# Token combinations of a first pass moved from one place in every step to two of three steps and into the downs, their low halves from GpSimd to VectorE

## The reference

```
x = x + tanh(g_ffn[0]) * _L0_ffn_ref(_layernorm(x, axis=-1), g_codes, g_absmax, ..., d_lora_b)

DM, DFF, R = (1024, 2752, 16)
w = NF4[codes].reshape(o, i // BLOCK, BLOCK) * absmax[:, :, None]      # Wg, Wu, Wd
y1 = x1 @ Wg + x1 @ g_lora_a @ g_lora_b
y2 = x1 @ Wu + x1 @ u_lora_a @ u_lora_b
x3 = jax.nn.relu(y1) * y2
y3 = x3 @ Wd + x3 @ d_lora_a @ d_lora_b
```

## Time and profile before

| | |
|---|---|
| time, median of 3 runs | 2003.04 us (2002.95 to 2003.74) |
| the profiled execution | 2003.48 us, span 2001.5 us |
| TensorE busy | 1918.8 us, 96% of the span |
| VectorE, ScalarE, GpSimd busy | 65%, 63%, 42% |
| granted TensorE clock, mean | 0.989 |
| HBM traffic | 303 MB, 151 GB/s |

### The profile page before, as it was taken

The page is one execution under the profiler, slowest core; times in us unless marked ns, Lnnn a source line. Parts: engine busy times, 40 slices in busy tenths (PEclk is TensorE's granted clock), DMA queues, the critical chain, the costliest instruction groups (busy, mean ns, idle before and its releaser), DMA issues. The chain is left out here.

```text
span 2001.5 us, 26467 instructions
## 1 busy us (share of the span) xinstructions
PE 1918.8 (96%) x9140; PEld 963.6 (48%) x9140; DVE 1293.8 (65%) x2204; ACT 1254.9 (63%) x1998; POOL 835.4 (42%) x752
## 2 busy tenths in 40 slices
PE   6996888999999999999999999999998899999998
PEld 5774334444444444444444445444444455555554
DVE  5776888364564736555473644636379988888872
ACT  6995668886777677676777776677524343443431
POOL 2443884222223223232232333222268667667742
PEclk9997998999999999999999999999999999999999
DMA  5651545856637375573737556373531110111001
GB/s 201 223 171 55 193 163 195 292 193 215 232 122 265 105 257 190 178 249 127 265 109 252 192 172 227 99 253 117 210 137 59 32 41 29 53 53 38 27 22 42
DMA packets 91989, 303.01 MB, mean 151 GB/s; under 512 B 11984, under 2 KB 16720, under 8 KB 73168
## 3 DMA queue, kind: packets, MB, share of 16 engines
q1 hardware_dynamic: 91856, 301.32, 44.3%
HBM read 274.01 MB, written 27.26 MB: 151 GB/s over the span
## 5 line engine op out<-in xcount | busy, mean ns | idle before, releaser
L1036 ACT ACTIVATE first<-first 128x512 f32<-128x512 int32 x1008 | 625.7, 626 | 27.4 <-DVE wt L1439 1.8
L1265 POOL TENSOR_TENSOR gu<-wt,gu 128x512 f16<-128x512 f32 x86 | 102.3, 1190 | 370.6 <-ACT gu L1055 370.5
L1439 DVE SCALAR_TENSOR_TENSOR wt<-first,w_scale,absm 128x512 f32<-128x512 f32 x132 | 102.6, 777 | 227.4 <-ACT first L1036 226.8
L1785 PE MATMUL a_psQ<-z,gu 128*128 128x512 f16 x936 | 208.5, 379 | 0.0
L2386 PE MATMUL a_psL<-z,l_x 128*128 128x512 f16 x768 | 170.7, 379 | 1.0 <-DVE l_x L2488 0.8
L1785 PE MATMUL a_psC<-z,gu 128*128 128x512 f16 x732 | 167.8, 379 | 0.0
L1785 PE MATMUL a_psC<-z 128*128 128x512 f16 x684 | 156.9, 379 | 0.0
L1785 PEld LDWEIGHTS a_psQ<-z,gu 128*128 128x128 f16 x936 | 91.5, 98 | 110.5
L1277 POOL TENSOR_TENSOR hid_lo<-z,hid_hi 128x512 f16<-128x512 f32 x76 | 90.2, 1201 | 118.7 <-ACT hid_hi L1096 118.6
L1265 POOL TENSOR_TENSOR dn_lo<-wt,dn_hi 128x512 f16<-128x512 f32 x42 | 50.3, 1197 | 199.2 <-ACT dn_hi L1055 199.2
L1442 DVE SCALAR_TENSOR_TENSOR wt<-a_psE,lora_gain,wt 128x512 f32<-128x512 f32 x132 | 99.1, 751 | 44.6 <-PE a_psE L1747 24.4
(11 more groups left out here) (418 smaller groups left out, 4122.3 us busy)
## 6 DMA issues: line engine op xcount, KB each, us to landing
z<-x_parts SPq DMA_DIRECT2D x140, 1024.0 KB, 5.8
first<-in_codes SPq DMA_DIRECT2D x132, 256.0 KB, 3.0
absm<-in_absmax SPq DMA_DIRECT2D x264, 128.0 KB, 3.3
X<-in_x SPq DMA_DIRECT2D x16, 512.0 KB, 4.3
c_in<-in_ctx SPq DMA_DIRECT2D x16, 512.0 KB, 5.3
cT<-in_ctxT SPq DMA_DIRECT2D x16, 512.0 KB, 3.6
o_sp<-in_w SPq DMA_DIRECT2D x16, 512.0 KB, 4.8
z<-in_ctx SPq DMA_DIRECT2D x8, 1024.0 KB, 7.0
```

Source lines behind the costliest of these rows:

```text
L1036: act.activation(level[w % 2][:], codes[w % RING] if k == 0 else level[w % 2][:], ACT.Prelu, bias=bias, scale=scale, alpha=alpha).then_inc ...
L1265: pool.tensor_tensor(low, source, high, ALU.subtract).then_inc(wlo_done, 1)
L1439: dve.scalar_tensor_tensor(wt[at], source[:], w_scale[:, m:m + 1], absm[w % RING][:], ALU.mult, ALU.mult).then_inc(scaled, 1)
L1785: mm = pe.matmul(out, w[:, k * P:(k + 1) * P], xx[:, k], start=first and q == 0, stop=q == 3 * KD // 2 - 1, skip_group_check=True)
```

## The change

`folding(s)` now gives ten parts to the steps 1, 2, 4, 5, 7, 8, 10, 11, 13 and 14, and the last six to the steps 16 to 21. The low halves of combinations (`fold_lo`) leave POOL's list and stand in DVE's, each pair at the head of the next folding step (`lows_after`), the last pair in step 22. They now count on the same semaphore as DVE's other folding operations, so that waits between the two engines go away; `fold_begin` stays on POOL with a semaphore of its own. SP stores the parts of a pair in the step in which DVE makes its low halves, and starts three of the five first token blocks of the second pass in step 22 in place of 20.

```
-            i, part = divmod(s - 1, 2)
-            return (i, part) if 0 <= i < B else None
+            order = [t for t in range(1, 16) if t % 3] + list(range(16, 22))
+            return divmod(order.index(s), 2) if s in order else None
...
+        def lows_after(m):
+
+            return (2 * m - 2, 2 * m - 1) if m else ()
...  SP
-                    if folding(s - 1):
-                        i, part = folding(s - 1)
-                        for k in range(2):
-                            store_part(4 * i + 2 * part + k)
+                    if folding(s):
+                        i, part = folding(s)
+                        for n in lows_after(2 * i + part):
+                            store_part(n)
+                    if s == 22:
+                        for n in lows_after(2 * B):
+                            store_part(n)
...
-                    if s == 20:
+                    if s == 22:
                         for c in range(2):
                             sp.wait_ge(prod_mm[c], 8)
                         wait_parts(4 * B)
...  POOL
-                def fold_lo(n):
-
-                    i, k = divmod(n, 4)
-                    pool.wait_ge(hi_done, TILES + n + 1)
-                    pool.tensor_tensor(folded_part(n, 1), fold(i, k % 2), folded_part(n, 0), ALU.subtract).then_inc(low_fold, 1)
...
-                        for k in range(2):
-                            fold_lo(4 * i + 2 * part + k)
...  DVE
+                def fold_lo(n):
+
+                    i, k = divmod(n, 4)
+                    dve.wait_ge(hi_done, TILES + n + 1)
+                    dve.tensor_tensor(folded_part(n, 1), fold(i, k % 2), folded_part(n, 0), ALU.subtract).then_inc(fold_done, 1)
...
                     if folding(s):
                         i, part = folding(s)
+                        for n in lows_after(2 * i + part):
+                            fold_lo(n)
                         (fold_first, fold_second)[part](i)
+                    if s == 22:
+                        for n in lows_after(2 * B):
+                            fold_lo(n)
```

More of the change, by code:

```diff
@@ L693, in phase_nf4_ffn @@
         hi_done, parts_out, blocks_out = res["hi_done"], [sem(f"parts_out{s}") for s in range(STAGES)], sem("blocks_out")
-        fold_done, low_fold = sem("fold_done"), sem("low_fold")
+        fold_done, begin_fold = sem("fold_done"), sem("begin_fold")
         copied, aside_done = sem("copied"), sem("aside_done")
@@ L784, in folding, with folded_no @@
         def folding(s):
-            i, part = divmod(s - 1, 2)
-            return (i, part) if 0 <= i < B else None
-        def begun(i):
-            return 6 * i - 2 if i else 2
+            order = [t for t in range(1, 16) if t % 3] + list(range(16, 22))
+            return divmod(order.index(s), 2) if s in order else None
+        def folded_no(i, what):
+            return 11 * i + {"T1": 1, "T2": 3, "T3": 7, "T4": 9}[what]
         def lows(i, k):
-            return 6 * i + k + (5 if i < B - 1 else 3)
+            return 11 * i + (4, 5, 10, 11)[k]
+        def lows_after(m):
+            return (2 * m - 2, 2 * m - 1) if m else ()
         def x_block(i, f, r, h):
@@ L946, in store_part @@
                     i, k = divmod(n, 4)
-                    sp.wait_ge(low_fold, lows(i, k))
+                    sp.wait_ge(fold_done, lows(i, k))
                     sp.dma_start(res["x_parts"][i // QUARTS, X_ORDER.index(FOLDS[k])][:, i % QUARTS, :], stage[n % STAGES]).then_inc(parts_out[n % STAGES], 16)
@@ L1114, in fold_hi @@
                     i, k = divmod(n, 4)
-                    act.wait_ge(fold_done, 7 * i + (1, 3, 5, 7)[k])
+                    act.wait_ge(fold_done, folded_no(i, FOLDS[k]))
                     if n >= STAGES:
@@ L1312, in fold_begin @@
                     if i > 1:
-                        pool.wait_ge(low_fold, lows(i - 2, 3))
+                        pool.wait_ge(fold_done, lows(i - 2, 3))
                     difference = fold(i, 0)
-                    pool.tensor_tensor(difference, x_block(i, 0, 1, 0), x_block(i, 0, 0, 0), ALU.subtract).then_inc(low_fold, 1)
-                    pool.wait_ge(low_fold, begun(i) - 1)
-                    pool.tensor_tensor(difference, difference, x_block(i, 0, 1, 1), ALU.add).then_inc(low_fold, 1)
-                def fold_lo(n):
-                    i, k = divmod(n, 4)
-                    pool.wait_ge(hi_done, TILES + n + 1)
-                    pool.tensor_tensor(folded_part(n, 1), fold(i, k % 2), folded_part(n, 0), ALU.subtract).then_inc(low_fold, 1)
+                    pool.tensor_tensor(difference, x_block(i, 0, 1, 0), x_block(i, 0, 0, 0), ALU.subtract).then_inc(begin_fold, 1)
+                    pool.wait_ge(begin_fold, 2 * i + 1)
+                    pool.tensor_tensor(difference, difference, x_block(i, 0, 1, 1), ALU.add).then_inc(begin_fold, 1)
                 def first_step(s):
@@ L1656, in hidden_first @@
                     dve.scalar_tensor_tensor(rel[:, n % 2, :], first_bank(n, 1), hid_gain[:], rel[:, n % 2, :], ALU.mult, ALU.mult).then_inc(fix_done[c], 1)
+                def fold_lo(n):
+                    i, k = divmod(n, 4)
+                    dve.wait_ge(hi_done, TILES + n + 1)
+                    dve.tensor_tensor(folded_part(n, 1), fold(i, k % 2), folded_part(n, 0), ALU.subtract).then_inc(fold_done, 1)
                 def fold_first(i):
-                    dve.wait_ge(low_fold, begun(i))
+                    dve.wait_ge(begin_fold, 2 * i + 2)
                     dve.tensor_tensor(fold(i, 0), fold(i, 0), x_block(i, 0, 0, 1), ALU.subtract).then_inc(fold_done, 1)
-                    dve.wait_ge(fold_done, 7 * i + 1)
-                    if i:
-                        dve.wait_ge(low_fold, lows(i - 1, 2))
+                    dve.wait_ge(fold_done, 11 * i + 1)
                     dve.tensor_tensor(fold(i, 1), x_block(i, 1, 1, 0), fold(i, 0), ALU.subtract).then_inc(fold_done, 1)
-                    dve.wait_ge(fold_done, 7 * i + 2)
+                    dve.wait_ge(fold_done, 11 * i + 2)
                     dve.tensor_tensor(fold(i, 1), fold(i, 1), x_block(i, 1, 1, 1), ALU.add).then_inc(fold_done, 1)
                 def fold_second(i):
-                    dve.wait_ge(low_fold, lows(i, 1))
-                    dve.wait_ge(fold_done, 7 * i + 3)
+                    dve.wait_ge(fold_done, lows(i, 1))
                     dve.tensor_tensor(fold(i, 0), fold(i, 1), x_block(i, 0, 0, 0), ALU.subtract).then_inc(fold_done, 1)
-                    dve.wait_ge(fold_done, 7 * i + 4)
+                    dve.wait_ge(fold_done, 11 * i + 6)
                     dve.tensor_tensor(fold(i, 0), fold(i, 0), x_block(i, 0, 0, 1), ALU.subtract).then_inc(fold_done, 1)
-                    dve.wait_ge(fold_done, 7 * i + 5)
+                    dve.wait_ge(fold_done, 11 * i + 7)
                     dve.tensor_tensor(fold(i, 1), x_block(i, 1, 0, 0), fold(i, 1), ALU.subtract).then_inc(fold_done, 1)
-                    dve.wait_ge(fold_done, 7 * i + 6)
+                    dve.wait_ge(fold_done, 11 * i + 8)
                     dve.tensor_tensor(fold(i, 1), fold(i, 1), x_block(i, 1, 0, 1), ALU.add).then_inc(fold_done, 1)
```

## The result

The changed kernel is slower, by twice as much as forecast. Median of four runs 2022.39 us (2018.21 to 2024.81), the kernel before in the same comparison 2003.39 us (2002.95 to 2006.21, four runs): ratio 1.009, interval 1.007 to 1.011. The prediction had 2012.6 with a range from 2001 to 2019. The profiled execution took 2024.81 us with a span of 2022.9 us, 21.4 more than the 2001.5 of before.

A forecast was written before the change was run, and what follows sets the result against it. A loop of DVE, ACT and POOL was taken to pace the turns. With 11.0 us gained there, the second pass starts 8.6 us later; plus 1.0 for the snapshot, 9.6 us slower: 2012.6 us, range 2001 to 2019.

The forecast's parts named there:

- The turns: Steps 1 to 15 of the first pass: last hidden product at 292.9 instead of 303.87, 11.0 us gained.
- The wait at the third turn: PE's 6.9 us wait in the first pass: moved, not gone, PE released at 226.1 instead of 227.50.
- the one at the fifth down: PE's 8.2 us wait in the first pass, claimed to shrink to some 4 us.
- The downs: Steps 16 to 22: folding added where DVE has no idle time; second pass at 354.9 instead of 346.25, 8.6 us lost.
- The sum of 61.3 us: Last hidden product to 28th drain: 52.45 us of DVE work, 8.3 stretching, 0.5 decode wait, against 37.9 before.
- ten stretched operations: DVE operations in steps 16 to 21 slowed beside POOL's, 10 x 0.83 = 8.3 us.
- One wait for a decode behind the high halves, 0.5: Downs: DVE waits just once for ACT's decode, 0.5 us of the sum.
- The snapshot: Opening of the second pass: ACT's second snapshot 16.9 us after the start, PE needs it at 15.8; 1.0 us wait.
- hidden, with 2 to 3 us to spare: Three x blocks moved to step 22: landed before the first is needed, 10.6 us after the second pass's start.
- Half the stretching: Rival: five stretched operations fewer in downs and as many in turns, 4 us back each, 2004.5 us; chance 0.20.
- none: Rival: no operation stretched, no decode late, second pass at 337.2, 9 us early, 1994 us; chance 0.12.
- The clock: Rival: PE stays at 1.2 GHz through the 28 downs behind the fifth, second pass at 363.2, 2020.9 us; chance 0.10.

The follow-up runs named there:

- e1: The changed kernel with the two LoRA rows of the next pass issued in step 22 ahead of the three x blocks instead of behind them; 2014.99 us.
- e2: The changed kernel with the first two x blocks (2 MB) of the second pass issued in step 15 instead of 18; 2015.57 us.
- e3: The changed kernel with x blocks 0 and 1 issued in step 15 and the LoRA rows ahead of the other three blocks; 2009.85 us.
- e4: The kernel before with the three x blocks of the second pass issued in step 22 instead of 20, right ahead of the LoRA rows; 2006.22 us.
- e7: The changed kernel with POOL's two operations that begin a batch on 8 columns instead of 512, all but the first two batches; 2016.61 us.
- e10: The kernel before's folding order with low halves shared, every second one on POOL and the others on DVE; 1999.79 us.
- e6: The changed kernel with folding order and x blocks' step as in the kernel before, low halves on DVE, last pair in step 17; 2002.34 us.
- e8: The changed kernel with DVE's folding operations of steps 16 to 22 on 8 columns instead of 512; 2002.55 us.
- e5: The kernel before with the new order of folding steps and x blocks in step 22, low halves left on POOL; 2019.56 us.

## Why the prediction was wrong

- **The turns: right.** Hidden products forecast at 211.2, 223, 236.3, 244.7, 256.6, 271.6, 280.3 and 292.9 came at 211.00, 222.76, 235.81, 243.75, 256.70, 270.98, 278.93 and 291.38. That the first one fits to 0.2 us is partly luck: in e1, e2 and e3, with the same turns, it came at 209.4 to 210.4. What carries is the length, 81.7 us forecast and 80.4 measured. The wait at the third turn stayed (6.0 us), the one at the fifth down fell to 3.4 (forecast 4).
- **The downs: mechanism right, one term missing.** The sum of 61.3 us: DVE's own work, its ten stretched operations and the start 0.65 us later gave 61.95; e3, without the late stores, has 62.9. What failed is the sentence "One wait for a decode behind the high halves, 0.5". There was one of 5.86 us, for a store behind 2 MB; in e2, with the 2 MB elsewhere, it was 0.66. The sum had not asked what stands ahead of the moved stores in SP's queue. This term put the start of the second pass at 358.27 instead of 354.9, although the last hidden product came 1.5 us early.
- **The snapshot: mechanism right, size wrong.** "With the scaling at about 6.4 us after the start it comes near 16.9: a wait of 1.0 us" carried over the 7.0 us from issue to use. It became 12.9 once 3 MB stood ahead, though the scaling came at 5.8, even a little early. Measured 6.87 + 2.5 for the low clock behind it + 0.4 around, 9.8 for 1.0. The sentence on the x blocks, "hidden, with 2 to 3 us to spare", was right and asked the wrong question: they were not late themselves, they made others late. e1 and e4 show it; only the size is open, since the same order gave waits from 2.9 (e2) to 6.9 us.
- **The rivals.** Half the stretching and none: refuted by the ten stretched operations; e7 shows that they are POOL's doing. The clock: from 291 to 358 us the granted clock was 0.82, and it came back between the waits, so this rival did not occur as told. PE's matmuls of the downs took 6 us more than before (46.4 for 40.3), but DVE waited for none of them in that stretch, so they lengthened nothing; the low clock took part as 2.5 us behind the snapshot. That the measured time lies near this rival's 2020.9 is chance.
- **Sum.** 3.4 us at the start and 8.8 behind it make 12.2 us, all but 0.1 of what the profile (21.9) has over the forecast (9.6). By the medians the miss is 9.8 us (2022.39 for 2012.6). e3, with both terms out, stands 5.6 us above before by the ratio and 4.8 by the medians, where 9.6 were forecast, 1.0 of them for the snapshot; its turns were 1.6 us shorter than forecast and began 1.8 us earlier, its downs 0.9 longer.

## What to carry to other kernels

When a change moves a transfer, ask not only whether it is still in time but which small transfers now stand behind it in its queue, who waits for these, and how full the DMA engines are there; a landing time read beside other neighbours doesn't carry over. Work moved into a stretch where its engine has no idle time costs nearly its full length there: here VectorE's busy time rose by 21.9 us in the downs, which became 24.5 longer, one wait of 5.9 among them, and fell by 13.6 in the turns, for 11.6 gained. Where two engines are near their bound in turn, sharing an operation between them can bring what moving it from one to the other doesn't: 5 us in e10, 2 to 3 in e6.

## What the runs showed of the hardware

In e8 DVE's operations of 8 columns took 0.17 us alone and over 1 us beside POOL. DVE and POOL of that kernel:

```profile
310.96 1.15 POOL L1324 TENSOR_TENSOR first<-first,z 128x512 f32<-128x512 f32 x1
311.01 1.12 DVE L1678 TENSOR_TENSOR o_sp<-o_sp,z 128x8 f32<-128x8 f32 x1
312.07 1.16 POOL L1272 TENSOR_TENSOR gu<-wt,gu 128x512 f16<-128x512 f32 x1
312.17 1.08 DVE L1680 TENSOR_TENSOR o_sp<-o_sp,z 128x8 f32<-128x8 f32 x1
...
314.40 0.17 DVE L1684 TENSOR_TENSOR o_sp<-o_sp,z 128x8 f32<-128x8 f32 x1
```

Each ends within 0.03 us of POOL's operation (312.11 and 312.13, 313.23 and 313.25). These operations of DVE, with two inputs in SBUF and begun later than POOL's, waited until POOL's had ended, though they are small; with a bandwidth shared in halves 8 columns would have been done in a fraction of this. The Trainium skill (SBUF — State Buffer, section Who interferes with whom) says this: a DVE instruction with two SBUF inputs and a GpSimd instruction that reads SBUF contend for a port pair that is an exclusive lock, and issue order decides who blocks. The trace agrees, and this also explains, where the operation that began 0.3 us ahead kept its 0.69 us. It goes the other way too: a POOL operation of this kernel that began at 309.28, while DVE's sum from 309.12 to 309.87 ran, took 1.60 us instead of 1.15. The drains, one of whose inputs lies in PSUM, weren't stretched: in the kernel after, the four from 317.05 to 319.76 came at their usual 0.66 us each, though POOL ran two operations from 316.54 to 319.38.

PE's wait and the clock behind it did not go in step. The 12 matmuls behind the wait for the snapshot took 5.28 us after 6.87 us of waiting (after, granted clock 0.50), 4.40 after 5.31 (e7, 0.61), 5.24 after 3.82 (e5, 0.52), 4.21 after 2.56 (e4, 0.65), but 2.75 after 2.88 (e2, 1.00).

That the small transfers were late behind the large ones fits a sentence of the Trainium skill (DMA: Bandwidth & Descriptors, section Two DMAs through the same engine are not ordered): within one queue of a DMA engine descriptors start in order. e1 and e4 agree: the same two rows took 4.8 and 5.9 us to landing ahead of the blocks (e1), 8.9 and 12.2 behind them (after), 5.1 and 6.4 with the blocks long landed (before), 8.9 and 11.5 with the blocks put right ahead of them (e4).
